# A four-layer graph network on one core: the high part ahead of the next sums in the first product, the last scores on TensorE, input tiles between strips, and clears of semaphores inside blocks

## The reference, cut to what matters

```python
    HW = jnp.einsum('bnf,fo->bno', H, W)
    A_norm = jax.nn.relu((A + A.T) * 0.5)
    D = jnp.sum(A_norm, axis=1)
    D_safe = jnp.where(D > 0, D, 1.0)
    d_inv_sqrt = jnp.where(D > 0, D_safe ** (-0.5), 0.0)
    DAD = d_inv_sqrt[:, None] * A_norm * d_inv_sqrt[None, :]
    L_norm = jnp.eye(N, dtype=H.dtype) - DAD
    out = jnp.einsum('nm,bmo->bno', L_norm, HW)
    return jax.nn.relu(out)
...
    Wh = jnp.einsum('bnf,fo->bno', h, W)
    a1, a2 = (a[:Fout, 0], a[Fout:, 0])
    s1 = Wh @ a1
    s2 = Wh @ a2
```

## Time and profile before

| what | us |
|---|---|
| median of three runs | 3167.99 |
| the profiled execution | 3172.0 |
| its span, first to last instruction | 3170.0 |
| `degrees`, to its last VectorE instruction's end | 86.3 |
| first product, from its first matmul to the last projection's start | 105.5 to 560.1 |
| attention's first products | from 625.8 |
| TensorE busy in the whole span | 2761.3 (87%) |
| VectorE, ScalarE, GpSimd busy | 1669.0, 1316.9, 172.3 |

### The profile page before, as it was taken

One profiled execution on the slowest core, in us unless ns is written; L12 is line 12 of the kernel. 1 busy time (PEld: TensorE's weight loads), 2 busy tenths in 40 slices (PEclk: granted clock), 3 DMA queues, 4 the chain that ended last, 5 costly groups with the idle time before them and its releaser, 6 DMA issues. The chain is left out here.

```text
span 3170.0 us, 38600 instructions
## 1 busy us (share of the span) xinstructions
PE 2761.3 (87%) x14435; PEld 2322.2 (73%) x14435; DVE 1669.0 (53%) x3214; ACT 1316.9 (42%) x2137; POOL 172.3 (5%) x97
## 2 busy tenths in 40 slices
PE   6688889299999895999999999698989886999987
PEld 6467767299999884888887777486867675778743
DVE  7666546666766752321322221678787873331345
ACT  2663443455556542211211111666676664221235
POOL 2000000100110000000000000010101000000000
PEclk9999999699999997999999999899999997999998
DMA  8544344412222314322432221301211115331258
GB/s 332 156 132 148 127 135 154 162 41 67 67 68 81 93 41 164 102 73 61 137 100 70 70 71 32 123 14 40 70 42 49 43 53 186 117 93 50 87 190 289
DMA packets 241190, 327.24 MB, mean 103 GB/s; under 512 B 13905, under 2 KB 155249, under 8 KB 236145
## 3 DMA queue, kind: packets, MB, share of 16 engines
q1 hardware_dynamic: 234096, 303.91, 29.8%
q10 hardware_dynamic: 6912, 20.97, 1.7%
HBM read 228.22 MB, written 96.62 MB: 102 GB/s over the span
## 5 line engine op out<-in xcount | busy, mean ns | idle before, releaser
L922 PE MATMUL l_acc<-l_a_hi,l_g_hi 128*128 128x512 f32 x1536 | 602.3, 392 | 48.9 <-DVE l_g_lo L853 39.7
L922 PE MATMUL l_acc<-l_a_lo,l_g_hi 128*128 128x512 f32 x1536 | 599.2, 390 | 0.0
L922 PE MATMUL l_acc<-l_a_hi,l_g_lo 128*128 128x512 f32 x1536 | 598.8, 390 | 0.0
L845 DVE TENSOR_TENSOR l_a_lo<-l_raw,l_a_hi 128x512 fp32r<-128x512 f32 x192 | 132.8, 692 | 771.0 <-ACT l_a_hi L795 771.0
L1279 PE MATMUL n_acc<-n_hb,n_p 128*128 128x129 f32 x4096 | 484.2, 281 | 46.9 <-DVE n_u L1237 30.9
L1279 PEld LDWEIGHTS n_acc<-n_hb,n_p 128*128 128x128 f32 x4096 | 478.1, 197 | 48.4 <-issue 27.9
L795 ACT ACTIVATE l_a_hi<-l_raw 128x512 fp32r<-128x512 f32 x192 | 121.2, 631 | 853.6 <-PE l_acc L922 817.2
L922 PEld LDWEIGHTS l_acc<-l_a_hi,l_g_hi 128*128 128x128 f32 x1536 | 289.3, 188 | 111.0 <-DVE l_g_lo L853 40.0
L1861 ACT ACTIVATE r_gate<-r_ps,r_bias 128x512 f32<-128x512 f32 (+2 forms) x504 | 297.6, 639 | 107.6 <-PE r_ps L2002 75.1
L1220 DVE SCALAR_TENSOR_TENSOR n_p<-n_e,n_cols,c_mT 128x2048 f32<-128x2048 f32 x128 | 296.0, 2346 | 81.4 <-ACT n_e L1190 59.7
L922 PEld LDWEIGHTS l_acc<-l_a_lo,l_g_hi 128*128 128x128 f32 x1536 | 289.3, 188 | 61.1 <-issue 1.4
(11 more groups left out here) (225 smaller groups left out, 3761.1 us busy)
## 6 DMA issues: line engine op xcount, KB each, us to landing
l_raw<-in_adjT_dram SPq DMA_DIRECT2D x256, 256.0 KB, 2.8
l_raw<-in_rows_dram SPq DMA_DIRECT2D x64, 256.0 KB, 2.7
l_hraw<-h SPq DMA_DIRECT2D x32, 512.0 KB, 3.6
z<-l_res SPq DMA_DIRECT2D x64, 256.0 KB, 2.7
m_z<-z SPq DMA_DIRECT2D x16, 1024.0 KB, 5.3
l_xt<-in_x_dram SPq DMA_DIRECT2D x30, 512.0 KB, 3.7
d_xt<-in_x_dram SPq DMA_DIRECT2D x16, 512.0 KB, 9.8
x<-l_y ACTq DMA_DIRECT2D x16, 512.0 KB, 4.6
```

What stands on the lines that cost most here:

```text
L845: dve.tensor_tensor(a_lo[:, gp % RING], raw[:, gp % RING], a_hi[:, gp % RING].bitcast(F32), ALU.subtract).then_inc(a_low, 1)
L922: last = pe.matmul(acc[:, b], lhs[:, s, b * D:(b + 1) * D], rhs[:, gp % RING], start=(s == 0 and lhs is g_hi and rhs is a_hi), stop=(s == ...
```

## The change

- In the product's loop on ScalarE, `high(gp)` goes ahead of `total(gp + 2)`.
- In `degrees`, x tiles have 8 buffers and are loaded and measured in another order: three ahead of the first strip, then two behind each strip, until all 16 are there.
- For the four tiles of the last quarter, s1 and s2 come from TensorE: it turns h (8 transposes), ScalarE copies them out of PSUM, TensorE multiplies by `wacol`, the product of W and the two halves of a, a 128 x 2 column pair that `degrees` now makes. VectorE moves the results. SP, no longer ScalarE, stores x1 and h1 of these tiles.
- `retire` is gone. `finished` notes the semaphores that are over, GpSimd clears them at the start of its part of a later block (`clear`: in `laplacian`, in `attention_near`, in `spread`), `cleared` gives them back behind that block. `finished` is called behind `degrees`, at the start of `attention`, and behind it.

```diff
-    def retire(self):
-
-        with self.nc.Block() as block:
-            @block.gpsimd
-            def _(pool):
-                for sem in self.live:
-                    pool.sem_clear(sem)
-        for sem in self.live:
+    def finished(self):
+
+        self.over, self.live = self.live, []
+
+    def clear(self, pool):
+
+        for sem in self.over:
+            pool.sem_clear(sem)
+
+    def cleared(self):
+
+        for sem in self.over:
             self.nc.release_semaphore(sem)
-        self.live = []
+        self.over = []
...
-    XR = 3
+    XR = 8
+
+    order = [("x", 0), ("x", 1), ("x", 2)]
+    for t in range(T):
+        order += [("a", t)] + [("x", k) for k in (2 * t + 3, 2 * t + 4) if k < T]
...
-            for t in range(T):
-                sp.dma_start(up[:, cut(t)], up_d[:, cut(t)]).then_inc(a_in[t], 16)
-                sp.dma_start(lo[:, cut(t)], lo_d[:, cut(t)]).then_inc(a_in[t], 16)
+            for kind, t in order:
+                if kind == "a":
+                    sp.dma_start(up[:, cut(t)], up_d[:, cut(t)]).then_inc(a_in[t], 16)
+                    sp.dma_start(lo[:, cut(t)], lo_d[:, cut(t)]).then_inc(a_in[t], 16)
+                    continue
                 if t >= XR:
                     sp.wait_ge(stats_own, t - XR + 1)
                 sp.dma_start(xt[:, t % XR], x_tiles[t]).then_inc(x_in[t % XR], 16)
...
-            dve.wait_ge(wa_summed, 2)
-            dve.tensor_copy(keep["wa"][:, :, :], pw[:, :, :])
-            for t in range(T):
-                dve.wait_ge(a_in[t], 32)
-                dve.tensor_tensor(diag[:, t], up[:, UPPER[t]:UPPER[t] + P], ident[:, :], ALU.mult).then_inc(dia_own, 1)
-                dve.wait_ge(dia_own, t + 1)
-                dve.tensor_tensor(up[:, cut(t)], up[:, cut(t)], lo[:, cut(t)], ALU.add).then_inc(added, 1)
+            dve.wait_ge(wa_summed, 3)
+            dve.tensor_copy(keep["wa"][:, :, :], pw[:, 0:2 * D].rearrange("p (k f) -> p k f", f=D))
+            dve.tensor_copy(keep["wacol"][:, :], pw[:, 2 * D:2 * D + 2])
+            for kind, t in order:
+                if kind == "a":
+                    dve.wait_ge(a_in[t], 32)
+                    dve.tensor_tensor(diag[:, t], up[:, UPPER[t]:UPPER[t] + P], ident[:, :],
+                                      ALU.mult).then_inc(dia_own, 1)
+                    dve.wait_ge(dia_own, t + 1)
+                    dve.tensor_tensor(up[:, cut(t)], up[:, cut(t)], lo[:, cut(t)], ALU.add).then_inc(added, 1)
+                    continue
...
+            pe.matmul(pw[:, 2 * D:2 * D + 2], wct[:, :], acol[:, :], start=True, stop=True).then_inc(wa_summed, 1)
...
-            sp.wait_ge(rs_out, 16)
+            for t in range(T - CH, T):
+                sp.wait_ge(x_done, t + 1)
+                sp.dma_start(io["x1"][t].rearrange("p b f -> p (b f)"), y[:, t % CH]).then_inc(rs_out, 16)
+                sp.wait_ge(h_done, t + 1)
+                sp.dma_start(io["h1"][t], normal(t)).then_inc(rs_out, 16)
+            sp.wait_ge(rs_out, 16 + 32 * CH)
...
+                if t >= T - CH:
+                    return
...
                 if gp < T:
                     features(gp)
+                high(gp)
                 total(gp + 2)
-                high(gp)
                 if gp >= T and gp % T == FINISH:
...
+            def copy_turned(j):
+                act.wait_ge(h_turned, j + 1)
+                if j >= 2:
+                    act.wait_ge(dotted, j - 1)
+                act.activation(xt[:, j % 2], acc[:, 2 * j:2 * j + 2].rearrange("p a n -> p (a n)"),
+                               ACT.Copy).then_inc(h_copied, 1)
+
             finish(CH - 1)
+            act.wait_ge(rs_turned, 1)
+            act.activation(keep["rsT"][0:T, :], acc[0:T, 0, 0:P], ACT.Copy).then_inc(rs_copied, 1)
             for j in range(CH):
                 normalise(T - CH + j)
-            act.wait_ge(rs_turned, 1)
-            act.activation(keep["rsT"][0:T, :], acc[0:T, 0, 0:P], ACT.Copy).then_inc(rs_copied, 1)
+                if j:
+                    copy_turned(j - 1)
+            copy_turned(CH - 1)
...
-                score(T - CH + j)
+                dve.wait_ge(dotted, j + 1)
+                dots = acc[:, 2 * j, 0:2 * B].rearrange("p (b k) -> p b k", k=2)
+                for k, col in enumerate((keep["s1"], keep["s2"])):
+                    dve.tensor_scalar(col[:, :, T - CH + j:T - CH + j + 1], dots[:, :, k:k + 1], 1.0, None, ALU.mult)
...
+            def turn(j):
+                pe.wait_ge(h_done, T - CH + j + 1)
+                if j == 0:
+                    pe.wait_ge(rs_copied, 1)
+                for b in range(B):
+                    last = pe.transpose(acc[:, 2 * j + b // 4, b % 4 * P:(b % 4 + 1) * P], normal(T - CH + j)[:, b],
+                                        ident[:, :])
+                last.then_inc(h_turned, 1)
+
+            def dot(j):
+                pe.wait_ge(h_copied, j + 1)
+                for b in range(B):
+                    last = pe.matmul(acc[:, 2 * j, 2 * b:2 * b + 2], xt[:, j % 2, b * P:(b + 1) * P],
+                                     keep["wacol"][:, :], start=True, stop=True)
+                last.then_inc(dotted, 1)
+
+            for j in range(CH):
+                turn(j)
+                if j:
+                    dot(j - 1)
+            dot(CH - 1)
...
         degrees(prog, io, keep, up, lo, x, wa, wcT)
-        prog.retire()
+        prog.finished()
         laplacian(prog, io, keep, x, w0)
+        prog.cleared()
```

More of the change, by code:

```diff
@@ L90, in __init__ @@
     def __init__(self, nc, ctx):
-        self.nc, self.ctx, self.live = nc, ctx, []
+        self.nc, self.ctx, self.live, self.over = nc, ctx, [], []
     def sem(self, name):
@@ L207, in degrees @@
         pc = prog.ps(ctx, "d_pc", [P, 512])
-        pw = prog.ps(ctx, "d_pw", [P, 2, D])
+        pw = prog.ps(ctx, "d_pw", [P, 512])
         sem = lambda s: prog.sem(f"d_{s}")
@@ L310, in _ @@
             for k in range(2):
-                pe.matmul(pw[:, k], wide_a[:, k], wct[:, :], start=True, stop=True).then_inc(wa_summed, 1)
+                pe.matmul(pw[:, k * D:(k + 1) * D], wide_a[:, k], wct[:, :], start=True, stop=True)\
+                  .then_inc(wa_summed, 1)
+            pe.matmul(pw[:, 2 * D:2 * D + 2], wct[:, :], acol[:, :], start=True, stop=True).then_inc(wa_summed, 1)
             for t in range(T - 1):
@@ L352, in laplacian @@
         x_out, h_out = sems("x_out", CH), sem("h_out")
+        h_turned, h_copied, dotted = sem("h_turned"), sem("h_copied"), sem("dotted")
         own, deg_own, rs_turned, rs_copied, rs_out = sem("own"), sem("deg_own"), sem("rs_turned"), sem("rs_copied"), sem("rs_out")
@@ L494, in _ @@
                     normalise(gp // T * CH - CH + NORMALISE.index(gp % T))
+            def copy_turned(j):
[4 more added lines that the diff above has]
+                               ACT.Copy).then_inc(h_copied, 1)
             finish(CH - 1)
+            act.wait_ge(rs_turned, 1)
+            act.activation(keep["rsT"][0:T, :], acc[0:T, 0, 0:P], ACT.Copy).then_inc(rs_copied, 1)
             for j in range(CH):
                 normalise(T - CH + j)
-            act.wait_ge(rs_turned, 1)
-            act.activation(keep["rsT"][0:T, :], acc[0:T, 0, 0:P], ACT.Copy).then_inc(rs_copied, 1)
+                if j:
+                    copy_turned(j - 1)
+            copy_turned(CH - 1)
             for s in x_out:
-                act.wait_ge(s, 16 * CH)
-            act.wait_ge(h_out, 16 * T)
+                act.wait_ge(s, 16 * (CH - 1))
+            act.wait_ge(h_out, 16 * (T - CH))
         @block.gpsimd
         def _(pool):
+            prog.clear(pool)
             ln.pool_setup(pool)
@@ L724, in ended_at, with _ @@
             return gp // T - 1 if gp % T == RING - 2 and gp >= T else None
+        @block.gpsimd
+        def _(pool):
+            prog.clear(pool)
         @block.sync
@@ L2182, in network @@
             gscale=[P, T, B], gshift=[P, T, B],
-            deg3=[P, T], dinv3=[P, T], wa=[P, 2, D], s1=[P, B, T], s2=[P, B, T], bn1=[P, 2, 2 * T, 6]).items()}
+            deg3=[P, T], dinv3=[P, T], wa=[P, 2, D], wacol=[P, 2], s1=[P, B, T], s2=[P, B, T], bn1=[P, 2, 2 * T, 6]).items()}
         degrees(prog, io, keep, up, lo, x, wa, wcT)
-        prog.retire()
+        prog.finished()
         laplacian(prog, io, keep, x, w0)
+        prog.cleared()
         attention(prog, io, keep, wc)
-        prog.retire()
+        prog.finished()
         spread(prog, io, keep, "l2", [dict(kind="L2a", h=io["h2"], w=wg0, b=bg0),
                                       dict(kind="L2b", h=io["h2b"], w=wg1, b=bg1)])
+        prog.cleared()
         recurrences(prog, io, keep, dict(wih=wih, whh=whh, bih=bih, bhh=bhh))
```

## The result

The changed kernel takes **3084.06 us** in the median of four runs (3078.25 to 3086.18), the kernel before beside it 3170.51 (3166.99 to 3174.1): a ratio of 0.9723, with a 95% interval of 0.9706 to 0.974. The forecast was 3080, its range 3063 to 3120.

The account below looks back on a forecast made before the run. The product was held by a 5.99 us loop a piece (TensorE needs 5.46) and a 21.3 us join chain. Terms of -67.7, -7.5, -2.3, -9.0, -1.8 sum to -88.3: 3172.0 to 3083.7, less 4.0 gives 3080; range 3063 to 3120.

Parts of the forecast that it names:

- high part first: First product: high parts no longer wait behind a transfer two pieces ahead; 387.2 us instead of 454.9, -67.7.
- input tiles between strips: Degrees: TensorE's column sums end at 73.9 and `k_nhd` at 78.2, not 86.32; -7.5 us, bounds -3 and -13.5.
- first clearing block: Between `k_nhd` and the product's first load: dropping the block with 32 clears saves 2.3 us.
- second clearing block: Behind attention: dropping the block with 137 clears saves 9.0 us (8.7 + 0.3).
- scores on TensorE: Product's tail: TensorE's products replace 16 VectorE steps of 1.22 us; -1.8 us, bounds -8 and +8.
- 5.65 a piece: First quarter: the load loop closes over two pieces in 11.3 us, giving a quarter of 91.8, not 103.1.
- chain of joins: Quarters 2 to 4: join, normalise, high part, score, next join over three pieces; from 21.3 us to 17.6, some 18.3 with diagonals.
- the loop of single pieces: Product before the change: freeing the raw buffer, landing, sums, high part and `l_a_lo` take 5.99 us a piece, against TensorE's 5.46.
- Three of my signs: Signs of being right: TensorE over 97% busy in quarters, projections starting within 3 us, `k_nhd` ending near 79.
- the rival that the clock rises with the work: Column sums and tail products run at TensorE's higher clock: -13.5 and -8 instead of -7.5 and -1.8; 3069, chance 0.07.
- The wait did not change its name: Rival: ScalarE stops in `high` for TensorE's buffers or VectorE's sum, pieces stay near 5.99; -35.5, 3112, chance 0.2.
- Transfers did not stretch to 5.9 us: Rival: faster pieces stretch landing; at 5.9 us other gains are eaten, at 7 us the time is 3203; chance 0.02.

Follow-up runs that it names:

- only_high: The kernel before with only `high(gp)` moved ahead of `total(gp + 2)`; 3101.43 us, ratio 0.9784.
- changed_again: The changed kernel itself, measured a second time; 3086.38 us, ratio 0.9742.
- high_after_store: The changed kernel with only twelve high parts, those right behind a normalised tile in quarters 2 to 4, ahead of the sums; 3122.79 us, ratio 0.9853.
- other_input_order: The changed kernel with another order of x tiles and strips in `degrees`, and VectorE's aggregations behind the next strip's add; one run, 3080.1 us.

## Why the prediction was right, and where not

| term | forecast | measured |
|---|---|---|
| high part first | -67.7 | -68.3 (alone -66.5; undone +70.2) |
| first quarter | 91.8 | 95.4 |
| first change of quarter | 10.4 | 13.1 |
| quarters 2 to 4 | 89.0 each | 87.2 each |
| later changes | 9.0 each | 8.2 each |
| input tiles between strips | -7.5 | -3.2 |
| first clearing block | -2.3 | -2.3 |
| second clearing block | -9.0 | -9.0 |
| scores on TensorE | -1.8 | -2.1 (undone +2.1) |
| sum | -88.3 | -84.9 |

The median fell by 86.5 us, and the sum of the measured terms is 84.9. The first profile's span fell by 93.6; 4.8 of that is attention and 3.6 the last stage. No edit speeds these up: attention only gained clears on GpSimd, and `only_high`, without them, has 596.3 us too; and `changed_again` and the others show both to vary by as much. So 3078.25 is a lucky execution, and the 8.7 us beyond the terms need no other cause.

**High part first.** The mechanism is as told, but that the sum of 387.2 came out at 386.3 is luck: 6.3 us too little in the first quarter and its change, 7.0 too much in what follows. The term "5.65 a piece" of the first quarter was mis-sized: `l_a_lo` comes 12.0 us apart over two pieces (140.20, 152.22, 164.56, 176.62, 188.24), not 11.3, because from the raw buffer's release to the sums are 4.7 us there (140.88 to 145.60) where I took 3.9. So 15 pieces take 89.8 and not 86.3. The change behind it was 10.4 in the forecast and 13.1 in the trace. `finish` starts at 197.77, 3.1 us after TensorE has ended the quarter, as forecast; but the projection needs two of ScalarE's copies first and begins at 198.93, and then takes 8.8 us, where I had 7.4: behind the 4.3 us in which TensorE stood, the granted clock is 0.50 from 199 to 202. The later quarters lost all their stalls, where I had left 1.6 us in each; I had also started from 99 us a quarter, which only quarter 4 took before. The step on what holds them was half right: chain of joins, yes (17.6 to 18.3 forecast, 17.9 to 19.0 measured); that the loop of single pieces binds beside it, no, as `high_after_store` shows. Three of my signs did not come: TensorE is busy 95.3% of the first quarter, not over 97%; the first projection starts 4.3 us behind the quarter's end, not within 3; and `k_nhd` ends at 83.14, not near 79, of which the next paragraph speaks.

**Input tiles between strips.** This step failed. I had TensorE's last 90 passes start at 54.6, when strip 6 has landed, and end at 73.9; they start at 57.67 and, with a pause of 1.60 for strip 7, end at 78.79. A strip needs VectorE's add (54.73) and ScalarE's sums (56.26) before a pass can run, which are the 3 us; and the statistics of x tiles, with an aggregation of 2.2 us at 57.82, stand ahead of strip 7's add at 60.57. I had said that VectorE "measures x while it waits"; from 42 to 66 us it never waits. The result, -3.2, lies at the low bound that I had given. `other_input_order` bears out that the order costs it: with other places for the x tiles and the aggregations `k_nhd` ends 4.1 us sooner, though it does not tell these two apart.

**Clearing and scores.** The price of 0.063 us a clear held. So did 0.214 us a pass at the lower level of TensorE's clock, which these rows of the changed kernel show (windows, columns as above; the first two are the projection behind the first quarter, the last two the narrow products of the tail):

```profile
199.00:202.00 3.00, 3.00 (x14) 3.00 (x15) 1.11 (x3) 1.49 (x3) 0.00 (x0) 0.50 0.27 97
202.00:205.00 3.00, 3.00 (x28) 3.00 (x27) 0.00 (x0) 1.97 (x3) 0.00 (x0) 0.94 0.00 0
506.59:510.00 3.41, 3.41 (x18) 3.41 (x18) 0.00 (x0) 3.41 (x9) 3.33 (x3) 0.50 0.61 241
516.62:523.40 6.78, 6.78 (x33) 6.74 (x32) 0.24 (x2) 1.02 (x1) 0.00 (x0) 0.50 0.00 0
```

The projection's passes of 128 columns take 0.214 us at a granted clock of 0.50 and 0.107 at 0.94. The narrow products take 0.213 a pass (3.41 us for 16) at 0.50, and the last 32 of them stay at 0.50 through 6.8 us without a pause. The column sums run up to 15.52 us without a pause at 0.216 us a pass, the lower level again by their duration; the column reads 1.00 there, as it does over the first matmuls of the product. So the rival that the clock rises with the work falls in both places. What a narrow pass takes at the higher level no run shows.
By the Trainium skill, TensorE: Matmul & The Clock Gate, Part 1, activity releases the throttle; these rows of narrow passes do not agree. (That rival's time was added up wrong, too: 3079.7 less 6.0 and 6.2 is 3067.5, not 3069.)

**The other rivals.** The wait did not change its name: 82.2 us, not 194.1. The high part's new wait, 27.0 us for TensorE's buffers, comes only in quarters 2 to 4, where TensorE has work without a pause, and costs nothing. Transfers did not stretch to 5.9 us: from 99 to 190 us a piece from `adjT` takes 4.2 us from issue to landing in the median.

## What to carry to other kernels

On an engine with a hand-written order, put the step that has its data ahead of the step that waits for a transfer, and check the steps that stay in between: each one left inside the loop (here 3.17 us of features) is paid in every turn. A chain over several pieces need not be broken in every piece: here once in three pieces took away all but 1.5 to 2.5 us of the stalls in a quarter. Where an engine "has time to spare" in a stage, follow its queue to the instruction that the bound waits for: a share of idle time does not say that the idle time comes before that instruction. And a span is compared with a second execution of the same program before a few us of it are explained.

## What was not expected of the hardware

- GpSimd's power on 128x8 takes 2.54 us when VectorE works on 128x1024 at its start, and 1.64 with VectorE idle; the product behind it takes 1.00 beside such a VectorE instruction and 0.20 without.
- The granted clock at the end of attention differs between executions of one program, 0.78 and 0.60 over 30 us, and with it that stage by 4.6 us.
- TensorE's narrow passes (128x2) took 0.213 us each at a granted clock of 0.50 through 6.8 us of unbroken work.
- A block boundary with nothing in it costs 0.33 us, and a semaphore clear about 0.06 us.
